# Row-gather passes of a graph network: what TensorE waits for before each product

## The reference

```python
# layer 2: gather by src, weigh, sum at the other end
hidden = einsum('ni,oi->no', h, W) + b
x = x + segment_sum(edge_weight[:, None] * hidden[src2], dst2, num_segments=3125)
# layer 3: a linear map by edge type, summed at dst
feat = sum over t of where(etype == t, h[src] @ W_w[t], 0)
x = x + elu(segment_sum(feat, dst, num_segments=3125) + h @ W_res + b_res)
```

## Time and profile before

| | |
|---|---|
| median of three runs | 4255.19 us (4251.41 to 4256.34) |
| the profiled execution's own time | 4260.01 us |
| its span | 4257.9 us |
| TensorE granted clock, mean | 0.811 |
| TensorE busy | 3084.3 us (72%) |
| VectorE busy | 2570.6 us (60%) |
| GpSimd busy | 2086.2 us (49%) |
| first gather pass, first to last indirect DMA | 3166.3 to 3655.6 us |
| second gather pass, first to last indirect DMA | 3740.7 to 4231.4 us |

### The profile page before, as it was taken

The page is one execution under the profiler, slowest core; times in us unless marked ns, Lnnn a source line. Parts: engine busy times, 40 slices in busy tenths (PEclk is TensorE's granted clock), DMA queues, the critical chain, the costliest instruction groups (busy, mean ns, idle before and its releaser), DMA issues. The chain is left out here.

```text
span 4257.9 us, 76630 instructions
## 1 busy us (share of the span) xinstructions
PE 3084.3 (72%) x18633; PEld 2181.0 (51%) x18633; DVE 2570.6 (60%) x9518; ACT 1354.4 (32%) x2970; POOL 2086.2 (49%) x2123
## 2 busy tenths in 40 slices
PE   2388885669999998389999669999655445644444
PEld 2266663226666665267777447777433333433333
DVE  7688886996555462768888657777653333422223
ACT  0067885950111100245555335555330000200000
POOL 0477773000000000377777257777527777267776
PEclk8578997999999999599999789999865555755555
DMA  2112222000000001366666254444411111322212
GB/s 60 42 51 68 74 75 96 2 1 30 16 16 16 17 15 34 106 176 181 182 177 172 52 143 128 130 129 127 76 45 53 53 53 53 119 73 53 53 53 55
DMA packets 247907, 325.62 MB, mean 76 GB/s; under 512 B 77964, under 2 KB 159451, under 8 KB 246523
## 3 DMA queue, kind: packets, MB, share of 16 engines
q1 hardware_dynamic: 180922, 207.94, 15.9%
q0 software_dynamic: 66656, 113.74, 11.5%
HBM read 229.22 MB, written 92.26 MB: 76 GB/s over the span
## 5 line engine op out<-in xcount | busy, mean ns | idle before, releaser
L2557 PE MATMUL gat_acc<-gat_rows,gat_hot 128*128 x1664 | 485.9, 453 | 504.6 <-SPq L2524 302.7
L1008 PE MATMUL hop_p_a<-hop_h,adj 128*128 128x384 bf16 x4375 | 712.5, 327 | 0.0
L2557 PEld LDWEIGHTS gat_acc<-gat_rows,gat_hot 128*128 128x128 f32 x1664 | 380.5, 318 | 611.3 <-issue 609.3
L1008 PEld LDWEIGHTS hop_p_a<-hop_h,adj 128*128 (+1 forms) x4375 | 427.7, 98 | 284.4 <-issue 1.5
L1952 POOL DMA_INDIRECT lb_far<-far_rows,lb_idx x416 | 407.7, 980 | 197.1 <-issue 117.9
L1952 POOL DMA_INDIRECT la_far<-far_rows,la_idx x416 | 409.5, 984 | 154.3 <-issue 117.3
L2535 POOL DMA_INDIRECT gat_rows<-typed_rows,gat_idx x391 | 372.7, 953 | 203.0 <-DVE gat_idx L2565 84.2
L2535 POOL DMA_INDIRECT gat_rows<-hidden_rows,gat_idx x391 | 371.4, 950 | 190.8 <-DVE gat_idx L2565 72.0
L1668 POOL DMA_INDIRECT by_src_records<-scatter_rec,scatter_rank x375 | 378.1, 1008 | 133.9 <-issue 100.0
L2573 DVE TENSOR_SCALAR gat_hot<-iota_row,gat_tabs 128x128 f32<-128x128 f32 x416 | 149.8, 366 | 336.8 <-PE gat_acc L2557 322.2
L560 POOL DMA_INDIRECT mid_by_src_tab_rec<-by_src_records,by_src_off x4 | 4.0, 1002 | 708.6 <-POOLq L84 707.7
(11 more groups left out here) (521 smaller groups left out, 6417.1 us busy)
## 6 DMA issues: line engine op xcount, KB each, us to landing
edge_features<-emb_out SPq DMA_DIRECT2D x104, 256.0 KB
la_feat<-edge_features SPq DMA_DIRECT2D x104, 256.0 KB
edge_features<-la_out SPq DMA_DIRECT2D x104, 256.0 KB
lb_feat<-edge_features SPq DMA_DIRECT2D x104, 256.0 KB
la_place<-dst_row SPq DMA_DIRECT2D x104, 128.0 KB
lb_place<-dst_row SPq DMA_DIRECT2D x104, 128.0 KB
typed_rows<-gat_typed_row SPq DMA_DIRECT2D x25, 512.0 KB, 2.6
cells_tabs<-x0share_nodes SPq DMA_DIRECT2D x125, 64.0 KB, 1.8
```

The lines of the kernel that those rows point to most:

```text
L1008: ins = nc.tensor.matmul(p_a[(u.par + r) % 2][:, 0:3 * D], K.adj[:, s, bass.ds(u.t * P, P)], h3[r % 2][:, s, :, :].rearrange("p i d -> p ( ...
L2557: nc.tensor.matmul(acc[:, bass.ds(tile[u % LOADS], D)], hot[u % HOTS][:, :], rows[:, bass.ds(row[u % LOADS], D)], start=False, stop=True, ...
```

## The change

TensorE no longer waits for `s_here` at a value read from the table, but for the ring semaphore of the unit that has the pair's own number (and for the last unit, from pair 390 on). Both parts of that wait are constants of the program. With it go SyncE's loop that counted the units, the semaphore `s_here`, and the third table row's load on TensorE. The table itself is still made and loaded as before.

```diff
-    s_tab, s_idx, s_none, s_turn, s_hot, s_sum, s_out, s_here = (
-        ph.sem(v) for v in ("tables", "idx", "none", "turn", "hot", "sums", "out", "landed"))
+    s_tab, s_idx, s_none, s_turn, s_hot, s_sum, s_out = (
+        ph.sem(v) for v in ("tables", "idx", "none", "turn", "hot", "sums", "out"))
...
             end.load(sp)
-            for v in range(V):
-                sp.wait_ge(s_rows[v % RING], (v // RING + 1) * 16)
-                sp.sem_inc(s_here, 1)
             end.sync(sp)
...
                     row = values(1, u, 0, (RING - 1) * D, skip_runtime_bounds_check_because=BOUNDED)
-                    here = values(2, u, 1, V)
                 pe.wait_ge(s_hot, u + 1)
-                pe.wait_ge(s_here, here[u % LOADS])
+                v = min(u, V - 1)
+                pe.wait_ge(s_rows[v % RING], (v // RING + 1) * 16)
                 nc.tensor.matmul(acc[:, bass.ds(tile[u % LOADS], D)], hot[u % HOTS][:, :], rows[:, bass.ds(row[u % LOADS], D)],
```

## The result

The changed kernel took 4274.82 us, the median of five runs (4272.99 to 4280.78), against 4255.19 us before (five runs, 4251.41 to 4256.34). The ratio is 1.0052, with a 95% interval of 1.0037 to 1.0067: slower by 0.5%, 19.6 us, where 20.8 had been forecast. The profiled execution is the one of 4274.82 us; its span is 4272.7 us.

A forecast was written before the change was run, and what follows sets the result against it. GpSimd's rhythm was taken to bound the passes; longer tails of 11.3 and 10.6 us less 1.4 us gave 20.5 us, so 4280.5 for the profiled execution and 4276 for the median, range 4266 to 4288 for 8 in 10.

The forecast's parts named there:

- The bound: Gather passes: GpSimd's own rhythm of indirect DMAs, 0.30 us gaps included, sets the pace, some 490 us a pass.
- The 23 extra pairs: End of each pass: 26 pairs instead of 3 stand behind the last landing, with three block boundaries among them.
- The price of the drain: Work behind each pass's last landing: 12.5 us instead of 1.2 and 1.9, adding 11.3 and 10.6 us.
- rival 5: Both passes' tails end at the high clock, shortening only the last block: +17, so 4272 us; chance 30%.
- the 11 to 13 named as a sign: Expected in the profile after: 11 to 13 us from last landing to VectorE's first instruction of the closing part.
- the low clock: Main forecast for the drains: array at the low clock, 0.43 us a pair, loads beside products: 4276 us; chance 45%.
- Loads beside products: Drain: a block costs sequencer and array 3.4 us each, side by side; if added instead, together 3 us more a pass.
- rival 4: Longer tails, by loads in series (+26) or old 4.5 us boundaries (+38): 4281 to 4294 us; chance 15%.
- SyncE's hop: Between landing and product at each pass's end: removing it saves 0.1 us a tail, ends 0 and 0.25.
- The 1.4 us of L2782: Second pass: this VectorE instruction stretched one indirect DMA to 2.31 us; it now runs after all DMAs, saving 1.4 us.
- Rival 1: Body: GpSimd's gap is waiting for TensorE's late hand-over, so the change makes it faster, 4168 us; chance 3%.
- rival 3: Late body: GpSimd comes to wait for TensorE, 1 us x 80 if at each block, 4350 us; chance 3%.

The follow-up runs named there:

- count_late: Changed kernel's constant waits for pairs 0 to 287 only, then SyncE's count and third load as before; VectorE's subtraction moved early: 4262.14 us, 1.0000 of the kernel before.
- third_load_kept: Changed kernel with the third table row still loaded and checked at each block, its values unused: 4302.65 us, 1.0095 of the kernel before, chip 3.
- changed_again: The changed kernel itself, unaltered, as a control on chip 3: 4282.92 us, 1.0053 of the kernel before.
- half_shift: Changed kernel with pair u waiting for unit u - u//34, leaving 15 pairs behind the last landing: 5125.17 us, 0.9870 of the kernel before, chip 1.
- The padding run: Changed kernel with 19 already fulfilled waits a block written on the tables' semaphore: 4287.95 us, 1.0065 of the kernel before, chip 3.
- ahead_6: Changed kernel with pair u waiting for unit u + 6: 5708.67 us in one run on chip 2.

## Why the prediction was right

**The bound.** Right: GpSimd's gap stayed at 0.30 us (in the changed kernel 597 waits put down to TensorE, none over 0.3), and count_late shows the change to be worth nothing in the body either way.

**The 23 extra pairs.** Right, and tested with count_late: take them away and the 20 us go (in the first pass there are 24 extra, 26 against two).

**The price of the drain.** 12.5 us from the landing were forecast; from the first of the 26 pairs to the closing part it took 10.5 and 10.6 us (3656.62 to 3667.14, 4240.30 to 4250.94), against a forecast 12.35. The mis-sized term is the array's pace at the end: 24 pairs took 8.7 us and not 10.6. The first two blocks are as forecast, 6.6 us against 3.4 + 3.4 (4242.07 to 4248.65; the sequencer's first loads start at 4240.6, 4243.9 and 4247.1, 3.3 and 3.2 us apart). The last block took 2.2 us and not 3.0 + 0.8: it went at the array's fast pace. That is the shape of rival 5, whose +17 kept the sequencer's blocks and shortened the last one alone. From the landing to the closing part's first instruction it is 10.9 us (4240.05 to 4250.94), just below the 11 to 13 named as a sign. Both drains ended at the high clock, as rival 5 had it. The granted clock in the two halves of each:

```profile
3658.40:3662.00 3.60, 3.57 (x17) 3.58 (x17) 2.27 (x7) 0.00 (x0) 0.00 (x0) 0.50 0.00 0
3662.00:3667.00 5.00, 4.95 (x33) 4.68 (x32) 2.95 (x10) 0.00 (x0) 0.00 (x0) 0.81 0.00 0
4242.00:4246.00 4.00, 3.93 (x18) 3.94 (x19) 2.11 (x8) 0.00 (x0) 0.00 (x0) 0.50 0.00 0
4246.00:4251.00 5.00, 4.73 (x32) 4.35 (x30) 4.27 (x11) 0.00 (x0) 0.00 (x0) 0.84 0.00 0
```

The columns are the stretch, its length, the busy time of TensorE's array, its weight loads, VectorE, ScalarE and GpSimd, and then the granted clock. The array is busy almost throughout, at the low level (0.50, 1.2 GHz) in the first half, and part of the second half is at the high level (2.4 GHz), which gives the means of 0.81 and 0.84. I gave that rival 30% and the low clock 45%: the wrong order. Its +17 is near the 17.7 that the two tails make in the profile with the 1.4 us by which GpSimd's second span is shorter. The medians came nearer to my sum for a reason that isn't in it: the last landing of the second pass took 3.28 us against 2.71, GpSimd's first span was 1.3 us longer, and the runs spread over 8 us. That 20.8 was forecast and 19.6 measured is therefore luck in part.

**Loads beside products.** Right: with 24 pairs in 8.7 us and two boundaries among them, no boundary can be added to the products. In the list of the drain's instructions they show as idle time of the array only in front of pair 392, and from the start of pair 390 to that of pair 392 it is 1.77 us (4240.30 to 4242.07), where 0.235 + 1.5 was forecast. third_load_kept bears out rival 4's price too: with the old boundaries the loss is 40 us, for which the prediction had +38.

**SyncE's hop.** I took 0.1 us off; it is nothing. Between landing and product lie 0.24 us without SyncE (4240.05 to 4240.30; 0.25 in changed_again) and 0.25 with it.

**The 1.4 us of L2782.** The cause is right: the instruction, L2779 in the changed kernel, stands at 4248.77, behind all DMAs, and the longest indirect DMA instruction of the pass takes 1005 ns and not 2312. That the full 1.4 us came back is not shown. The second span is 489.3 us here, but 489.5 to 490.7 in the four kernels of chip 3, which have no stretched instruction either; before it was 490.7. The instruction ended at 4250.79, 0.15 us ahead of the closing part, so it only just fits beside the last products.

**Rival 1** (the hand-over is the bound) was given 3% and is false here. On chips 1 and 2 its outcome holds by a different mechanism, a sequencer that stops: kernels of the changed form gain 1.2 to 1.4% there. The trace of one chip could not have told that.

Two more numbers of the prediction need a word. Its rival 3 writes 4350 for 80 times 1 us, which would be 4356. And the median of 4255.19 us before, called that of three runs ahead of the prediction, stands over all five.

What stays open is the cause of those stops. Dearer register work alone is not enough, since half_shift has no checked load and its passes still take 554 and 553 us. Nor is a chip that is slow throughout: the hops' matmuls take 326 ns on both kinds, and that stage 712 us (1420.4 to 2132.8 on chip 2, 975.8 to 1688.0 before). The Trainium skill ("Runtime: NRT & Kernel Launch", "Instruction fetch mechanics") says that code is fetched in blocks of 256 instructions, mostly hidden. Code that comes late is a guess that would fit stops in long unrolled stretches and their growth with the number of instructions. In the second pass, q8 of the instruction queues has 13 packets on chip 2 and 14 in the kernel before (q14 has 12 in both), so no more code is fetched there. Whether it comes late, no run here shows. The padding run might have helped to tell, but it ran on chip 3.

## What to carry to other kernels

Before a wait is made simpler by making it later, count what stands behind its last event: in the body a later wait is free as long as the engine that waits isn't the one that sets the pace and doesn't come to hold it up (ahead_6 shows where that ends), and at the end each instruction that could have been done before is paid in full (here 24 and 23 pairs, 19.1 us, so some 0.4 us a pair). If the simple form is wanted, keep the exact wait for the end only, from where the engine can still catch up. A fall of an engine's idle time is no gain by itself, since work that is done piece by piece can fill it (here 126 us less idle, 145 us more busy). And idle time tells where the slack is on the chip of the trace; on another chip, where the kernel before takes 23% longer, its passes were held up by the engine that idles here.

## What the runs showed of the hardware

- Two of the three chips of the experiments ran this program in 5195 and 5235 us instead of 4255 to 4263. In the gather passes there, TensorE's array has gaps of up to 15 us, and in the one shown above single register instructions and checks of its sequencer take up to 0.7 us instead of 0.02 to 0.15. On both kinds of chip the hops' matmuls take the same 326 ns.
- Register loads of eight values take 589 ns and of four 334 ns (medians), and they run beside products that are still in the array (a load and the last pair's product both start at 4206.4).
- From a DMA's landing to the start of a product that waits for it alone it took 0.24 us, no sooner than through SyncE's wait and count (0.25 us).
- 19 waits in a row on one semaphore became 8 instructions, some 0.11 us of the sequencer each.
- A pair of f32 matmuls alone took 0.79 us at the low clock, one in a burst 0.43.
- A drain of 24 pairs without a gap began at a granted clock of 0.50 and had 0.81 and 0.84 in its second half; its last eight pairs took 2.2 us.
